# A fused Mamba-style block and expert network: the scan re-laid on the partitions, prepared during the last batch, with softplus moved to GpSimd

## The reference

```python
def _L0_conv_ref(x, ...):                      # x: (8, 256, 32, 32), 1024 tokens, fp32
    xz = silu(einsum('oc,bchw->bohw', in_proj_w, x) + in_proj_b)      # 768 x 256
    x_ssm, res, gate = split(xz, 3, axis=1)
    xf = silu(depthwise_conv3(x_ssm over the tokens) + dw_b)
    x_h = gather(xf as (8, 2 heads, 128, 1024), perm)   # order of tokens by a Mobius score, per head
    dbc = einsum('oc,bcn->bon', dbc_w, xf) + dbc_b      # per head 1 + 8 + 8 rows
    dt = softplus(dbc[:, :, 0]); B_t = dbc[:, :, 1:9]; C_t = dbc[:, :, 9:]     # gathered by perm
    A = -exp(A_log)                                     # (2, 8)
    # over the 1024 tokens, state h: (8, 2, 128, 8)
    #   h = exp(dt*A) * h + dt*B_t * x ;  y = sum_s h*C_t + D*x
    y = ungather(y, perm)
    y = y * silu(gate) + res
    return silu(einsum('oc,bchw->bohw', out_proj_w, y) + out_proj_b)

x = x + _L0_conv_ref(layernorm_over_channels(x), ...)
t = tokens of x                                  # (8, 1024, 256)
t = t + _L0_ffn_ref(layernorm(t), ...)           # softmax gate over 8 experts, threshold 0.1,
x = t as (8, 256, 32, 32)                        # renormalised; sum of weight_e * (t @ W_e + b_e)
```

## Time and profile before

| | us |
|---|---|
| median of 3 runs (lowest, highest) | 1158.37 (1156.52, 1159.8) |
| the profiled execution, its time | 1164.22 |
| its span | 1162.5 |
| PE busy in the span | 993.3 (85%) |
| DVE busy | 846.8 (73%) |
| ACT busy | 524.1 (45%) |
| POOL busy | 459.9 (40%) |
| mean granted clock of PE | 0.875 |

### The profile page before, as it was taken

One profiled execution on the slowest core, in us unless ns is written; L12 is line 12 of the kernel. 1 busy time (PEld: TensorE's weight loads), 2 busy tenths in 40 slices (PEclk: granted clock), 3 DMA queues, 4 the chain that ended last, 5 costly groups with the idle time before them and its releaser, 6 DMA issues.

```text
span 1162.5 us, 15111 instructions
## 1 busy us (share of the span) xinstructions
PE 993.3 (85%) x4482; PEld 736.1 (63%) x4482; DVE 846.8 (73%) x2105; ACT 524.1 (45%) x1050; POOL 459.9 (40%) x400
## 2 busy tenths in 40 slices
PE   5998888993478889888725999999999999999997
PEld 4876777873244445444413777777777777777776
DVE  5758776844389988988713877787777777877786
ACT  3766666762365675576503233333232333332331
POOL 2112222441378888878635333331323333142000
PEclk8998999896577677677756999999999999999999
DMA  6256554443323434333241314031131313022000
GB/s 184 110 127 178 145 142 102 135 125 105 102 59 99 110 91 116 91 103 103 56 145 36 127 38 144 31 109 59 39 123 36 144 36 127 38 76 103 0 19 37
DMA packets 77365, 108.97 MB, mean 94 GB/s; under 512 B 18394, under 2 KB 60676, under 8 KB 74244
## 3 DMA queue, kind: packets, MB, share of 16 engines
q1 hardware_dynamic: 70148, 90.37, 26.0%
q0 software_dynamic: 7168, 18.03, 5.5%
HBM read 60.46 MB, written 47.92 MB: 93 GB/s over the span
## 4 chain that ended last, share of the span: by engine, by line
PE 61%; DVE 12%; POOL 11%; issue 7%; DMA 4%; ACT 3%; another core or an unknown queue 1%; ACTq 0%; SPq 0%; DVEq 0%; POOLq 0%
PE bank L1180 28%; PE bank L1061 5%; PE bank L1096 4%; PE bank L959 4%; POOL stage L618 4%; PE bank L1064 4%; PE bank L1113 4%; PE bank L1051 3%; PE bank L1022 2%; PE bank L1141 2%; PE bank L969 2%; DMA score_scratch<-score 1%; POOL sp L554 1%; POOL dtri L602 1%; POOL xtm L657 1%
## 5 line engine op out<-in xcount | busy, mean ns | idle before, releaser
L618 POOL TENSOR_TENSOR stage<-stage,rg 128x512 f32<-128x512 f32 x112 | 142.2, 1269 | 62.5 <-DVE rg L1599 52.8
L657 POOL DMA_INDIRECT xtm<-y_scratch,idxu x128 | 127.7, 998 | 83.2 <-issue 36.2
L669 POOL TENSOR_TENSOR ssm<-ssm,rg 128x512 f32<-128x512 f32 x32 | 37.5, 1195 | 275.6 <-DVE ssm L1679 275.6
L1180 PE MATMUL bank<-wexph,xhl 128*128 128x512 f32 x512 | 144.9, 405 | 0.0
L1180 PE MATMUL bank<-wexph,cr 128*128 128x512 f32 x512 | 142.0, 399 | 0.9 <-DVE ysb L1783 0.8
L1180 PEld LDWEIGHTS bank<-wexph,xhl 128*128 128x128 f32 x512 | 93.8, 190 | 23.3 <-DVE xf L1783 2.1
L795 ACT ACTIVATE rg<-dist,acol 128x256 f32<-128x256 f32 x256 | 108.1, 524 | 0.0
L1180 PEld LDWEIGHTS bank<-wexph,cr 128*128 128x128 f32 x512 | 93.0, 188 | 22.4 <-DVE ysb L1783 3.4
L1599 DVE TENSOR_TENSOR rg<-rg,bank 128x512 f32<-128x512 f32 x128 | 84.4, 681 | 27.4 <-PE bank L1051 21.5
L1180 PE MATMUL bank<-wexpl,xhl 128*128 128x512 f32 x256 | 80.9, 397 | 0.0
L1180 PE MATMUL bank<-wexpl,cr 128*128 128x512 f32 x256 | 79.3, 391 | 0.0
(11 more groups left out here) (289 smaller groups left out, 2161.2 us busy)
## 6 DMA issues: line engine op xcount, KB each, us to landing
xin<-in_x SPq DMA_DIRECT2D x16, 1024.0 KB, 10.8
res_gate_scratch<-rg SPq DMA_DIRECT2D x16, 1024.0 KB, 4.0
rg<-res_gate_scratch SPq DMA_DIRECT2D x8, 2048.0 KB
rows_scratch<-stage SPq DMA_DIRECT2D x8, 1160.0 KB, 9.6
y_scratch<-ysb SPq DMA_DIRECT2D x16, 512.0 KB, 3.9
out<-stage SPq DMA_DIRECT2D x16, 512.0 KB, 2.8
bc_scratch<-r SPq DMA_DIRECT2D x16, 288.0 KB, 3.0
bl<-bc_scratch SPq DMA_DIRECT2D x16, 192.0 KB
```

The source lines that it names most:

```text
L618: pool.tensor_tensor(ksum, dskip.rearrange("p t n -> p (t n)") if s == 0 else ksum, ee[:, s, :], ALU.add).then_inc(summed.sem, 1)
L657: pool.indirect_dma_start(out=xtm[:, t, h * P:(h + 1) * P], out_offset=None, in_=y_d.rearrange("q s r c -> (q s r) c"), in_offset=bass.Ind ...
L1180: last = pe.matmul(bank[4 + i][:, :], x_[:, k, i * P:(i + 1) * P], w[:, 2 * ep * KC + k:2 * ep * KC + k + KC + 1:KC, :], start=(n + k == 0 ...
```

## The change

*Layout of the scan.* A partition now holds a head and one of 64 tokens; the free dimension holds two half blocks times 4 batches. `states` writes, in four groups of 32 rows, one 128x128 tile straight into a free part of `A_BANK`; `block_states` and the masks `bdm` are gone; `next_states` works on 64x128. `weigh` writes in eight pieces; `args` is 256 columns and keeps both heads (the other head's A is 0), its exponentials go to a second tile `argx`. As a partition has one head, `decays` is one instruction of 512 columns per state. The mask is added by PE behind `same` (`identr`, `bigr`, fp32r), so `masked` is gone. `y_of` is 16 pairs' matmuls of 128 columns. `y_scratch` is laid out by partition.

```diff
-            def states(c, y_before):
-                for h in range(HEADS):
...
-                    pe.matmul(bank[SY_BANK + h][:, :], bw[:, :, :]..., xr[c.four][:, h * GB:(h + 1) * GB, 0:P], ...)
+            def states(c):
+                pe.wait_ge(w_ready.sem, w_ready.at(c.q, 4))
+                pe.wait_ge(a_free.sem, a_free.at(c.q, 2))
+                pe.wait_ge(h_ready.sem, h_ready.at(c.q, 0))
+                for g in range(4):
+                    rows = slice(PART * g, PART * (g + 1))
+                    for e in range(2):
+                        last = pe.matmul(bank[A_BANK][rows, 3 * P:4 * P], bw[:, e, rows], xr[c.four][:, 2 * g + e, 0:P], ...)
 def rows_of(c):
+                if c.q:
+                    pe.wait_ge(h_ready.sem, h_ready.at(c.q - 1, 2))
...
                 pe.matmul(bank[B_BANK][:, :], same[:, :], dtri..., start=True, stop=False)
+                pe.matmul(bank[B_BANK]..., identr[:, :], bc(bigr[:, :], 1, ST), start=False, stop=True)
 def y_of(c):
+                for high in range(2):
+                    for i in range(2):
+                        wait for y2_half[i] if high else y2_used[i]
+                        for e in range(2):
+                            b, g = 2 * high + e, 2 * i + high
+                            rows = slice(PART * g, PART * (g + 1))
+                            dst = bank[SY_BANK + i][:, b * P:(b + 1) * P]
+                            pe.matmul(dst, cwt[c.four][rows, e, :], hs[c.four][rows, :], start=True, stop=False)
+                            last = pe.matmul(dst, kbd[:, GB * i + b, :], xr[c.four][:, GB * i + b, 0:P], ...)
 DVE weigh(c)
+                for h in range(HEADS):
+                    for w, part, i in ((bw, 0, 1), (cw, 1, 0)):
+                        for e in range(2):
+                            last = dve.tensor_tensor(dst, src[:, e], by[:, e], ALU.mult)     # 64x32 each
```

```diff
+            def softplus_front(b):      # after neg_ready
+                power; +2; power -1; *; square                          # 5 dependent, 128x16
+            def softplus_back(b):
+                1 + 5 x 2 + 3 dependent operations on 128x16, then 2 additions and 2 products into the staging tile
 POOL
             for b in range(NB):
+                if b:
+                    softplus_front(b - 1)
                 if b + 1 < NB:
                     deviations(b + 1)
+                if b:
+                    softplus_back(b - 1)
+                if 1 <= b <= WEXP_PARTS:
+                    low_experts(b - 1)
+                if b == NB - 3:
+                    scatter_order(0)
                 if b == NB - 2:
                     scatter_order(1)
+            wait for the order, for all rows of batches 0 to 6, for the transposes of the last batch
             for q in range(4):
                 gather_rows(Chunk(q))
+            up_to_token(Chunk(0))
+            softplus_front(NB - 1)
+            softplus_back(NB - 1)
             up_to_token(Chunk(1))
             chunks(body)
-            RANKS = {1: (0, 2), 2: (2, 6), 3: (6, 10), 4: (10, 13), 5: (13, 16)}
+            RANKS = {2: (0, 4), 3: (4, 8), 4: (8, 12), 5: (12, 16)}
```

*The scan prepared in the last batch*:

```diff
 PE batch(b)
                 in_proj(b, par, 5, MI)
+                if not ahead:
+                    pe.wait_ge(rows_staged.sem, rows_staged.at(b - 1, 4))
+                    sums_of(Chunk(0))
+                    rows_of(Chunk(0))
                 rows_by_tokens(b)
 DVE, after batch(7)
+            memset cr[0]; flatten(0); exponents(0); distances(0)
+            dbc_in(NB - 1); rows_low(0); weigh(0)
+            memset cr[1]; memset hs[0]; flatten(1); exponents(1); next_states(0)
 SP: turn is loaded at the start of batch 7, store_rows(7) stands in body(0)
```

More of the change, by code:

```diff
@@ L169, in metaformer @@
         cs = sb("cs", [P, 2, ST])
-        args = sb("args", [P, 2, S * ST])
+        args = sb("args", [P, 2, ST, HEADS * S])
+        argx = sb("argx", [P, 2, ST, HEADS * S])
         dtri = sb("dtri", [P, ST, SUB])
-        dist = [sb(f"dist{i}", [P, ST, SUB]) for i in range(2)]
+        dists = sb("dists", [P, 2, ST, SUB])
+        dist = [dists[:, i, :, :] for i in range(2)]
         ee = rg[:, :, :].rearrange("p a n -> p (a n)").rearrange("p (s n) -> p s n", s=S)
[L174 to L179, removed]
+        dskip = sb("dskip", [P, ST, SUB])[:, :, :]
+        bw = sb("bw", [P, 2, P])
+        cw = sb("cw", [P, 2, P])
+        cwt = [sb(f"cwt{i}", [P, 2, P]) for i in range(4)]
         dec = sb("dec", [P, 1])
@@ L622, in body @@
                 c = Chunk(q)
-                add_state(c, 0)
-                if q + 1 < CHUNKS:
-                    masked(Chunk(q + 1))
-                for s in range(1, S - 1):
+                for s in range(S - 1):
                     add_state(c, s)
@@ L1045, in products @@
+                for g in range(4):
+                    rows = slice(PART * g, PART * (g + 1))
+                    for e in range(2):
+                        last = pe.matmul(bank[A_BANK][rows, 3 * P:4 * P], bw[:, e, rows], xr[c.four][:, 2 * g + e, 0:P],
+                                         start=(e == 0), stop=(e == 1))
+                last.then_inc(st_full.sem, 1)
             def products(c, lo, hi):
@@ L1481, in batch @@
                 if b:
-                    dbc_chain(b - 1)
+                    dbc_in(b - 1)
                 convolve(b, 0)
@@ L1498, in batch @@
                     places()
[L1499 to L1528 removed]
             def flatten(c):
[L1533 removed]
+                dve.wait_ge(xr_ready[c.four].sem, xr_ready[c.four].at(c.turn4, 32))
                 if c.q:
@@ L1632, in body @@
                 whole_kernel(c)
-            dve.wait_ge(cr_zero, 3)
+            determinant()
+            front = Steps(dve, dve1, 0)
+            statistics(front, 0)
+            high_weights()
+            normalised(front, 0)
+            low_weights_of_all()
+            low_parts(0, 0)
+            dve.wait_ge(pads_done, 2)
+            for b in range(NB):
+                batch(b)
+            for k in range(2):
+                dve.wait_ge(mm_full[k].sem, mm_full[k].at(NB - 1, 0))
+            dve.memset(cr[0].bitcast(F32), 0.0).then_inc(cr_zero, 1)
             first = Chunk(0)
@@ L1638, in _ @@
             distances(first)
+            dbc_in(NB - 1)
             rows_low(first)
             weigh(first)
-            next_states(first)
+            for i in range(2):
+                dve.wait_ge(mm_full[i].sem, mm_full[i].at(NB, 0))
+            dve.memset(cr[1].bitcast(F32), 0.0).then_inc(cr_zero, 1)
+            dve.memset(hs[0][0:SUB, :], 0.0).then_inc(cr_zero, 1)
+            dve.wait_ge(kbd_zero, 1)
+            dve.wait_ge(cr_zero, 3)
             flatten(Chunk(1))
             exponents(Chunk(1))
+            next_states(first)
             chunks(body)
```

500 lines of the change are left out of this document (243 added, 257 removed).

## The result

| | before | after |
|---|---|---|
| median (lowest, highest) of 4 runs each | 1157.79 (1156.52, 1159.8) | 1232.21 (1229.73, 1234.07) |
| span of the profiled execution | 1162.5 | 1228.0 |
| PE busy | 993.3 | 1079.6 |
| mean granted clock of PE | 0.875 | 0.806 |

The change makes the kernel slower: the ratio of the times is 1.064, with a 95% interval of 1.061 to 1.0669. 1140 was forecast, and the range of 1108 to 1164 does not hold the time.

The account below looks back on a forecast made before the run. PE was taken to wait for DVE's normalised x in the batches and to follow a 17.07 us loop through POOL in the scan; -24.5 + 9 - 11 + 8 = -18.5 on 1164.2, less 5.8, gave 1140, range 1108 to 1164.

Parts of the forecast that it names:

- Batches 1 to 5: First stage: softplus on POOL ends PE's wait for normalised x, 33 to 27.5 us a batch, -24.5 in all.
- jam of 3 us on SP: Batch 2: SP sends score rows, staged rows and residual one behind the other, 3 us given back.
- Batch 6: Normalisation's power on POOL comes late, behind the scatter and softplus; PE waits, +9 us (bounds 0 and +13).
- Preparation: Part 2, scan prepared in the last batch: second `same` 40 instead of 51.6 us after the projections, gain 11 (0 to 20).
- The chunk: Scan: only additions to the 17.07 us loop, +0.5 a chunk, +8 over 16 chunks (bounds 0 and +27).
- Part 3: The forecast's part on the scan chunk: one state tile, mask moved to PE, `y_of` in 16 matmuls; +8 us in all.
- 0.2 net for both with the mask: Scan chunk: mask matmul and re-cut `y_of` of the same 2048 columns add 0.2 us (bounds 0 and 1.1).
- the wait of `rows_of`: Scan chunk: `rows_of` waits for the previous chunk's state update behind a wider `args` on DVE, 0.3 us more (0 to 0.6).
- Rival (b): Scan: PE's clock stays low because half of `y_of` uses 32 rows; +34 instead of +8, 1166 us; chance 0.15.
- Rival (a): POOL is not late in batch 6 and the scan loop does not grow; preparation -16, 1118 us; chance 0.25.
- Rival (c): Softplus on POOL costs twice the price, 0.6 us a step, in batch 6 and preparation; 1152 us; chance 0.1.
- The expert stage: Behind the scan: left alone by the change apart from the addresses of its gathers.

Follow-up runs that it names:

- e7: e6 with products 4 and 5 issued before `y_of` and ACT's output copies behind all decays; 1125.91 us, ratio 0.9711 to the kernel before.
- e9: e7 with POOL's normalisation power for batch 7 moved ahead of the first part of softplus of batch 5, in batch 6; 1126.87 us, ratio 0.9718.
- e1: Changed kernel with the state part of `y_of` on all 128 rows instead of 32 (another output); 1126.83 us.
- e5: Changed kernel with the eight 32-row state matmuls of `y_of` first, then the eight 128-row ones, nothing left out; 1127.94 us, ratio 0.9726.
- e4: Changed kernel with DVE running `next_states` before `exponents`, so `sums_of` instead of `rows_of` waits for the state update; 1196.89 us.
- e6: e5 and e4 together: grouped `y_of` matmuls and the state update before the next chunk's sums; 1127.75 us, ratio 0.9723.
- e2: Changed kernel with the kernel part of `y_of` also on only 32 rows, leaving out three quarters of its sum over tokens; 1127.76 us.
- e8: Changed kernel with the state part of `y_of` on 64 rows instead of 32 (another output), same matmul order; 1233.35 us.
- e10: e9 with `dtri` of chunk 0 right behind the first gather, ahead of the gathers of chunks 1 to 3; 1119.96 us, ratio 0.9667.

## Why the prediction was wrong

**Batches 1 to 5: right, and undersized.** -24.5 was forecast; `rows_by_tokens` of batch 5 starts at 181.6. In the kernel before it starts at 212.1, one batch of the same 33.4 behind the 178.8 of the earlier trace rows. That is -30.5. The jam of 3 us on SP that I gave back in batch 2 is nowhere (76.35 to 102.15 is 25.8). The 27.5 a batch was right: in e7, whose first stage is the same, the five take 27.4 to 27.6 each, with a granted clock of 0.94. In the profiled execution of the changed kernel three of the five take 25.8 to 26.0 at a clock of 1.00, and two 27.6. The 4.7 us between the two go with the clock, and the forecast had no term for them. One reading in the forecast is off: the stretch 188.34 to 194.3 is 6.0 us, not about 5.

**Batch 6: right.** +9 was forecast. It lasts 218.4 - 181.6 = 36.9 us, where it took 240.9 - 212.1 = 28.8: +8, by the mechanism named, the normalisation's power behind the scatter and a power of softplus. What e9 adds is that this term and the next aren't independent. The stall lies beside a chain on POOL that decides the start of the scan anyway; taking it away made batch 6 7.2 us shorter and gave 0.6 at the second `same`.

**Preparation: right.** -11 was forecast for the stretch, -8.8 measured (31.3 in all, less the 22.5 gained up to batch 6). The order of the steps, and the last softplus at 12.5 us (271.44 to 284.09, 12.65), came as described. The small steps of softplus took 0.21 to 0.28 plus a turn of 0.08, against my 0.3 with the turn. On the Trainium skill's rule that two-input elementwise work takes GpSimd about twice VectorE's time (GPSIMD Engine Reference, "Engine selection"): the same product on the same tile, on DVE before and on POOL in the changed kernel, took 175 and 230 ns in the mean, so 1.3 times here, less than the rule gives.

```profile
L1419 DVE TENSOR_TENSOR sp<-sp 128x16 f32<-128x16 f32 x8 | 1.4, 175 | 0.3
```
```profile
L597 POOL TENSOR_TENSOR sp<-sp 128x16 f32<-128x16 f32 x40 | 9.2, 230 | 3.3
```

In batches 1 to 5 it cost nothing, as the forecast said.

Together -26.5 was forecast up to the second `same`, and -31.3 came.

**The chunk: here it failed, and by more than ten times.** +0.5 a chunk was forecast and 7.2 measured in the steady chunk (6.4 in the mean of 14), +8 against 104 us in all. Two steps of Part 3 are wrong.

The first is "`y_of` has the same 2048 columns ... so 0.2 net for both with the mask (bounds 0 and 1.1)". I counted columns and looked at the clock, and both halves of `y_of` had rows of their own to price them by, all of 128 rows. A matmul of 32 rows *between* two of 128 had none. I carried over the price of the nearest group without asking what it was next to. The trace of before did hold the price. Inside its `y_of` all matmuls use 128 rows, but the first state matmul stands behind the 48-row products and costs 2.00; the second stands behind matmuls of 128 rows and costs 1.71 at the same low clock:

```profile
508.96 1.71 PE bank L1061 x2
```

One change of range is 0.29 there. In the changed kernel a matmul of 128 columns costs 0.72 at the low clock instead of the 0.43 of e1: again 0.29, and 16 of them are 4.6 (15 are new). e5 takes 14 of the 16 changes away and regains it all, with the same instructions; in e7 `y_of` is 5.4 shorter at the same clock, because matmuls of 32 rows in different groups then also run side by side.

The second is "0.3 more (bounds 0 and 0.6)" for the wait of `rows_of`. I priced it as the delay of one DVE instruction beside a loop that POOL closes. Once PE's queue is the longer loop, it is the link that closes this loop. I can read its size in a chunk of e4 in which PE waits for none of it, 431.56 to 454.56: 23.0 instead of 24.3, so 1.3. e6 shows the other side: with POOL's loop back, the same edit is worth nothing, so the forecast's value held as long as its condition did.

What is left of the 7.2 is 23.0 - 4.6 = 18.4 against 17.07, 1.3: all of PE's work of a chunk at 1.2 GHz, mask included. The three shares are an estimate, worked out from chunks of different kernels, so each may be off by some tenths. In the three chunks in whose `y_of` the clock rose, the period was 2.6 shorter.

**Rival (b)** named the low clock (0.51, and 0.50 throughout 420 to 434) and the sign, and worked out 18.8 for a chunk on PE at 1.2 GHz, which the 18.4 bears out. Its cause is refuted by e2 and e8, and by e7, where half of `y_of` uses 32 rows and the scan has a clock of 0.66 (300 to 560; 0.69 before). Its `y_of` of 6.8 us misses the exposed loads, the largest share of the loss. It gave 1166, and 66 us are missing. Rival (a), whose -16 for the preparation had no working, was half right: the loop of 17.07 does absorb the mask and the smaller matmuls, as soon as the range stops changing (e1, e5). Rival (c) did not come.

The Trainium skill has the mechanism: TensorE: Matmul & The Clock Gate, Part 3, "The mechanism", says that PE pulls a weight load ahead of running matmuls when it goes to other row groups or to the background buffer. The trace agrees: e2, in which every second pair goes on to another group of 32 rows, starts matmuls of two groups within 0.01 us of each other (at 412.90), and e1, with 128 rows throughout, has its loads beside the matmul before (0.43 a matmul). That a load whose groups overlap the running matmul's only in part gets neither is what the rows here show (0.72); that section doesn't say it.

The expert stage was costed at nothing and is 7.5 shorter. 4.9 of it are fewer waits of PE for `xf` (12.2 us in six waits before, 7.3 in one after); why they are fewer stays open, and so does the rest.

## What to carry to other kernels

When a matmul is cut to fewer rows, price it by what stands before and behind it: alternating row ranges cost about one weight load each time (0.29 us here, at the low clock), and grouping the matmuls by range, with the accumulation left open between the groups, takes it away. A loop that holds its period to within 0.02 us (17.07 here) hides what lies beside it only until another loop through the same engines gets longer, so work out that second loop as a full sum, at the low clock, before costing additions at nothing. A stall is worth its length only if the chain that starts the next stage runs through it: e9 made a batch 7.2 us shorter and gained nothing measurable, while e10 moved one instruction of 1 us past six DMA issues and gained 6.9, 4.4 of it seen at its place.

## What was not expected of the hardware

- Between fp32 matmuls of 128 columns, a change of the row range (32 or 64 rows to 128 and back) makes one 0.72 us instead of 0.43 at a granted clock of 0.50, and 0.41 instead of 0.22 at 1.00. The load of 32 rows is not shorter than the one of 128 (291 and 295 ns over 300 to 560 of the changed kernel).
- Matmuls of 32 rows in different row groups run side by side. At a granted clock of 0.50 the 16 matmuls of `y_of` take 5.2 us with all of them on 32 rows (e2), 6.3 with half of them on 128 (e7), and 6.9 by the 0.43 of one on 128 rows (e1; 16 x 0.43).
- The clock stayed at 0.50 for 14 us in which PE showed no idle time (420 to 434 of the changed kernel, busy 14.00). It rose in 3 of the 16 `y_of` there and in 10 of 16 in e4, where the range alternates too, and in 7 of 16 in e2 and all 16 in e1, where it doesn't. So the alternation doesn't forbid the rise; whether it makes it rarer isn't shown. That the clock follows PE's busy time can't be read from these rows: the earlier trace rows show a rise while PE is busy, and these 14 us show none.
